# Cutting the second half's projection units and the first half's output units in two pieces, one beside each self-attention step

## The reference

```python
h = _rms(x, w_ln1)
q = (h @ wq + bq).reshape(B, S, N_HEADS, HEAD_DIM)
k = (h @ wk + bk).reshape(B, S, N_KV, HEAD_DIM)
v = (h @ wv + bv).reshape(B, S, N_KV, HEAD_DIM)
q, k = _rope(q, k)
scores = jnp.einsum('bqhd,bkhd->bhqk', q, k) * HEAD_DIM ** (-0.5)
scores = jnp.where(causal[None, None], scores, jnp.finfo(scores.dtype).min)
attn = jax.nn.softmax(scores, axis=-1)
ctx = jnp.einsum('bhqk,bkhd->bqhd', attn, v).reshape(B, S, N_HEADS * HEAD_DIM)
x = x + ctx @ wo
h = _rms(x, w_ln2).reshape(B * S, H)
logits = h @ w_router
```

## Time and profile before

| what | us |
|---|---|
| median of 3 runs | 965.73 |
| lowest and highest of them | 959.88, 966.84 |
| span of the profiled execution | 962.0 |
| TensorE busy with matmuls in it | 902.7 (94%) |
| VectorE, ScalarE, GpSimd busy | 635.9, 561.5, 401.5 |

### The profile page before, as it was taken

One profiled execution on the slowest core, in us unless ns is written; L12 is line 12 of the kernel. 1 busy time (PEld: TensorE's weight loads), 2 busy tenths in 40 slices (PEclk: granted clock), 3 DMA queues, 4 the chain that ended last, 5 costly groups with the idle time before them and its releaser, 6 DMA issues.

```text
span 962.0 us, 16220 instructions
## 1 busy us (share of the span) xinstructions
PE 902.7 (94%) x5759; PEld 836.1 (87%) x5759; DVE 635.9 (66%) x1438; ACT 561.5 (58%) x1448; POOL 401.5 (42%) x382
## 2 busy tenths in 40 slices
PE   5999999999999999999989889799998999998997
PEld 4889999999999999999867767598998888987997
DVE  3557777743537777761597965575866777978764
ACT  3666666754546667663335666545437767776761
POOL 3532222335442223245535323344224766676531
PEclk9999999999999999999999899799989989999999
DMA  5734710016540000005532112134376989998975
GB/s 154 210 88 115 212 51 2 12 39 173 153 125 1 17 1 2 1 12 144 143 94 56 44 48 53 37 98 124 101 250 188 299 244 287 296 303 271 285 191 156
DMA packets 112760, 122.20 MB, mean 127 GB/s; under 512 B 9887, under 2 KB 77927, under 8 KB 112680
## 3 DMA queue, kind: packets, MB, share of 16 engines
q1 hardware_dynamic: 97806, 98.80, 33.4%
q0 software_dynamic: 5184, 12.13, 6.1%
q10 hardware_dynamic: 9690, 10.24, 3.7%
HBM read 110.72 MB, written 19.07 MB: 135 GB/s over the span
## 4 chain that ended last, share of the span: by engine, by line
PE 68%; DVE 13%; DMA 10%; ACT 4%; issue 3%; POOL 2%; ACTq 0%; POOLq 0%; DVEq 0%; SPq 0%
PE bank L2068 61%; PE bank L2197 4%; DMA s_sum<-yo,target 2%; DVE we L1342 2%; DMA eraw<-in_L_ffn_w_up_e_dram 2%; DMA eraw<-in_L_ffn_w_down_e_dram 2%; DMA raw<-in_L_xattn_Wq_dram 1%; ACT we L915 1%; POOL wx L1909 1%; DMA sums<-s_sum 1%; PE bank L2374 1%; DVE PQ L1339 1%; DMA eraw<-in_L_ffn_w_gate_e_dram 1%; DVE wf L1342 1%; DMA raw<-in_L_xattn_Wo_dram 1%
## 5 line engine op out<-in xcount | busy, mean ns | idle before, releaser
L1938 POOL TENSOR_SCALAR SC<-SC,mx,anyv 100x361 f32<-100x361 f32 x128 | 81.8, 651 | 210.4 <-DVE mx L1454 200.6
L1909 POOL TENSOR_TENSOR wf<-raw,wf 128x512 fp32r<-128x512 f32 x54 | 71.6, 1333 | 111.4 <-ACT wf L901 111.4
L1909 POOL TENSOR_TENSOR wx<-raw,wx 128x512 fp32r<-128x512 f32 x64 | 83.4, 1313 | 75.5 <-ACT wx L901 75.2
L1342 DVE TENSOR_TENSOR we<-eraw,we 128x704 fp32r<-128x704 f32 (+2 forms) x100 | 92.1, 938 | 24.6 <-ACT we L915 24.5
L915 ACT ACTIVATE we<-eraw 128x704 fp32r<-128x704 f32 (+2 forms) x140 | 96.3, 718 | 19.9 <-DMA eraw<-in_L_ffn_w_down_e_dram 9.2
L1921 POOL TENSOR_TENSOR we<-eraw,we 128x704 fp32r<-128x704 f32 x40 | 76.3, 1908 | 54.5 <-ACT we L915 54.4
L2068 PE MATMUL bank<-H2h,wf 128*128 128x400 f32 x352 | 99.0, 347 | 0.0
L1031 ACT ACTIVATE SC<-SC,mx 100x361 f32<-100x361 f32 x128 | 75.4, 593 | 28.8 <-DVE mx L1450 27.9
L2068 PE MATMUL bank<-XTh,wx 128*128 128x400 f32 x256 | 71.6, 353 | 3.5 <-POOL wx L1909 2.1
L1342 DVE TENSOR_TENSOR Kl<-bank,Kh 128x362 fp32r<-128x362 f32 x64 | 34.1, 534 | 60.3 <-ACT Kh L989 60.3
L1342 DVE TENSOR_TENSOR QOl<-bank,QOh 128x200 fp32r<-128x200 f32 (+1 forms) x96 | 41.4, 432 | 47.3 <-ACT QOh L944 37.2
(11 more groups left out here) (282 smaller groups left out, 2769.0 us busy)
## 6 DMA issues: line engine op xcount, KB each, us to landing
raw<-s_unit SPq DMA_DIRECT2D x60, 256.0 KB, 3.1
eraw<-in_L_ffn_w_gate_e_dram SPq DMA_DIRECT2D x40, 352.0 KB, 3.9
eraw<-in_L_ffn_w_up_e_dram SPq DMA_DIRECT2D x40, 352.0 KB, 5.4
eraw<-in_L_ffn_w_down_e_dram SPq DMA_DIRECT2D x40, 256.0 KB, 5.9
raw<-in_L_xattn_Wq_dram SPq DMA_DIRECT2D x32, 256.0 KB, 3.0
raw<-in_L_xattn_Wo_dram SPq DMA_DIRECT2D x32, 256.0 KB, 3.0
eraw<-in_L_ffn_w_down_e_dram SPq DMA_DIRECT2D x20, 192.0 KB, 4.9
s_unit<-in_L_ffn_w_sh_gate_dram SPq DMA_DIRECT2D x11, 256.0 KB, 3.7
```

Source lines behind the costliest of these rows:

```text
L1342: return eng.tensor_tensor(o, src, f32(hi), ALU.subtract)
L1909: eng.tensor_tensor(w[:, 1, :, :], raw[plan.raw[stream, u] % 4][:, :, :], f32(w[:, 0, :, :]), ALU.subtract).then_inc(sem("pool_w"), 1)
L1938: eng.tensor_scalar(sc, sc, m[:, 3, h:h + 1], anyv[:, b:b + 1], ALU.mult, ALU.mult).then_inc(sem("pool_p"), 1)
```

## The change

The eight query and key units and the four value units of the second half, and the four output units of the first half, are each issued in two pieces: `..._begin` takes the weights and the bank and makes the first 6 of the 12 matmuls, the old name the other 6 and the signal. Only TensorE has work in the new steps. The pieces stand beside the attention steps like this: units 0 to 3 of query and key still whole behind steps 0 to 3 (the rope of the one before between the pieces); first pieces of units 4, 5, 6, 7 behind 4, 6, 8, 10, second pieces behind 5, 7, 9, 11; rope as before. Value units: first pieces behind 13, 15, 16, 18, second pieces behind 14, 15, 17, 19. Output units: first pieces behind 20, 22, 24, 26, second pieces behind 21, 23, 25, 27. The epilogue is moved and pressed together: `er` two behind 28 and two behind 29, `eroot` and two `erms` behind 30, `eh` behind 31, 32, 33 and 34, router product and first gate unit behind 34, so that only step 35 is left. The `fetch` steps of query and key units 4 to 7 stand one step earlier; those of the value units stand behind 13, 15 and (two) 19, instead of 13, 14 and (two) 17.

```diff
@@ steps_ffn
     at = [[("at", n)] for n in range(8 * HB + 4)]
-    qk = [g for n in range(8) for g in ([fetch, ("qk", 1, n)], [("rope", 1, n)])]
-    yield from take(at, 1)
-    yield from take(qk, 1)
-    for n in range(12):
+    qk = []
+    for n in range(8):
+        qk += [[fetch, ("qk_begin", 1, n)] + ([("rope", 1, n - 1)] if n else []), [("qk", 1, n)]]
+    qk.append([("rope", 1, 7)])
+    for n in range(13):
         yield from take(at, 1)
-        yield from take(qk, 2 if n < 3 else 1)
-    yield from take(qk)
-    v = [[("vbat", 0), fetch], [("vadd", 0), ("vbat", 1), fetch], [("vadd", 1), ("vbat", 2)], [("vadd", 2), ("vbat", 3)],
-         [("vadd", 3), fetch, fetch]]
-    for _ in range(5):
+        yield from take(qk, 2 if n < 4 else 1)
+    v = [[("vbat_begin", 0), fetch], [("vbat", 0)], [("vadd", 0), ("vbat_begin", 1), fetch], [("vbat", 1)],
+         [("vadd", 1), ("vbat_begin", 2)], [("vbat", 2)], [("vadd", 2), ("vbat_begin", 3)], [("vbat", 3)]]
+    for n in range(7):
         yield from take(at, 1)
-        yield from take(v, 1)
-    yield from take(at, 2)
-    po = [[fetch, ("po", 0, m)] for m in range(KD)]
+        yield from take(v, 2 if n == 2 else 1)
+    yield from (("vadd", 3), fetch, fetch)
+    po = [g for m in range(KD) for g in ([fetch, ("po_begin", 0, m)], [("po", 0, m)])]
     ep = epilogue_groups(0)
-    for _ in range(4):
+    for _ in range(8):
+        yield from take(at, 1)
         yield from take(po, 1)
+    for n in range(7):
         yield from take(at, 1)
-    for _ in range(9):
-        yield from take(ep, 1)
-        yield from take(at, 1)
+        yield from take(ep, 2 if n < 2 else 1)
     yield ("moe0",)
@@ tensor_program
+        def qk_begin(n):
+            w, bank = unit("f"), free_bank(("qk", 1, n))
+            begun.append((w, bank))
+            pe.wait_ge(sem("dve_ht"), B)
+            for k in range(2):
+                mm3(bank[:, 0:HT], w[:, 0, k, :], w[:, 1, k, :], HTh[1][:, k, :], HTl[1][:, k, :], k == 0, False)
+
+        def qk_end():
+            w, bank = begun.pop()
+            for k in range(2, KD):
+                e = mm3(bank[:, 0:HT], w[:, 0, k, :], w[:, 1, k, :], HTh[1][:, k, :], HTl[1][:, k, :], False, k == KD - 1)
             e.then_inc(sem("pe_qk"), 1)
+        def v_batch_begin(i):
...
+            v_part(i, bank, range(2))
+
+        def v_batch(i):
+            v_part(i, banks[plan.bank["vbat", i]], range(2, KD)).then_inc(sem("pe_fv"), 1)
+        def po_begin(m):
+            w = unit("f")
+            pe.wait_ge(sem("dve_cx"), HB)
+            bank = free_bank(("po", 0, m))
+            begun.append((w, bank))
+            po_part(0, w, bank, range(2))
```

More of the change, by code:

```diff
@@ L2272, in free_bank, with qk @@
             return banks[plan.bank[key]]
-        def qk(h, n):
+        def qk(n):
             w = unit("f")
-            pe.wait_ge(sem("dve_ht"), HB * (h + 1))
-            if h:
-                bank = free_bank(("qk", h, n))
-            else:
[L2280 to L2284, removed]
-            for k in range(KD):
-                e = mm3(bank[:, 0:HT], w[:, 0, k, :], w[:, 1, k, :], HTh[h][:, k, :], HTl[h][:, k, :], k == 0, k == KD - 1)
+            pe.wait_ge(sem("dve_ht"), HB)
+            bank = banks[n % 4]
+            if n >= 4:
+                pe.wait_ge(sem("dve_rope"), n - 3)
+            else:
+                pe.wait_ge(sem("act_yt"), KD + (n - 2) % 4 + 1)
+            for k in range(KD):
+                e = mm3(bank[:, 0:HT], w[:, 0, k, :], w[:, 1, k, :], HTh[0][:, k, :], HTl[0][:, k, :], k == 0, k == KD - 1)
+            e.then_inc(sem("pe_qk"), 1)
+        begun = []
+        def qk_begin(n):
[8 more added lines that the diff above has]
+                e = mm3(bank[:, 0:HT], w[:, 0, k, :], w[:, 1, k, :], HTh[1][:, k, :], HTl[1][:, k, :], False, k == KD - 1)
             e.then_inc(sem("pe_qk"), 1)
@@ L2306, in tensor_program, with v_part @@
         v_units = []
-        def v_batch(i):
+        def v_part(i, bank, ks):
+            ts = slice(i * T, (i + 1) * T)
+            for k in ks:
+                (name, value), w = v_units[k]
+                pe.wait_ge(sem(name), value)
+                e = mm3(bank[0:T, :], HTh[1][:, k, ts], HTl[1][:, k, ts], flat(w[:, 0, :, :]), flat(w[:, 1, :, :]),
+                        k == 0, k == KD - 1)
+            return e
+        def v_batch_begin(i):
             if i == 0:
@@ L2312, in v_batch @@
             bank = free_bank(("vbat", i))
-            ts = slice(i * T, (i + 1) * T)
             pe.wait_ge(sem("dve_ht"), B)
[L2315 to L2319, removed]
+            v_part(i, bank, range(2))
+        def v_batch(i):
+            v_part(i, banks[plan.bank["vbat", i]], range(2, KD)).then_inc(sem("pe_fv"), 1)
         def f_scores(q, pair):
@@ L2384, in self_attention, with po_part @@
                 f_scores(n // 4 + 1, 0)
+        def po_part(h, w, bank, ks):
+            for k in ks:
+                e = mm3(bank[:, 0:HT], w[:, 0, k, :], w[:, 1, k, :], CXh[h][:, k, :], CXl[h][:, k, :], k == 0, k == KD - 1)
+            return e
+        def po_begin(m):
[4 more added lines that the diff above has]
+            po_part(0, w, bank, range(2))
         def po(h, m):
+            if h == 0:
+                w, bank = begun.pop()
+                po_part(0, w, bank, range(2, KD)).then_inc(sem("pe_po"), 1)
+                return
             w = unit("f")
             pe.wait_ge(sem("dve_cx"), HB * (h + 1))
[L2389 to L2392, removed]
+            po_part(h, w, free_bank(("po", h, m)), range(KD)).then_inc(sem("pe_po"), 1)
         def er(h, i):
@@ L2542, in tensor_program @@
                 resid(*a)
+            elif name == "qk" and a[0] == 0:
+                qk(a[1])
+            elif name == "qk_begin":
+                qk_begin(a[1])
             elif name == "qk":
-                qk(*a)
+                qk_end()
             elif name == "rope" and a[0] == 0 and a[1] - 1 in BY_PE:
@@ L2548, in tensor_program @@
                 v_row(*a)
+            elif name == "vbat_begin":
+                v_batch_begin(*a)
             elif name == "vbat":
@@ L2552, in tensor_program @@
                 self_attention(*a)
+            elif name == "po_begin":
+                po_begin(a[1])
             elif name == "po":
```

## The result

| | before | changed |
|---|---|---|
| median of 20 runs, us | 966.18 | 969.62 |
| span of the profiled execution, us | 962.0 | 967.2 |
| ratio to before, 95% interval | | 1.0045 [1.0026, 1.0063] |

The change makes the kernel slower by 0.45%, some 4 us. I had forecast a gain of 2.8 us.

The account below looks back on a forecast made before the run. VectorE was taken to bound the rotary steps, two-step loops through ScalarE to set the pace after. Terms -7.6+0.6+4.2 gave -2.8 us, from a median of 965.73 to 963.0 us; range 956 to 971.

Parts of the forecast that it names:

- part 1: Query and key units, steps 0 to 12: VectorE stays the bound, halving them loses 0.6 us, bounds 0 and 1.8.
- Parts 2 and 3: Halved value and output units: steps 15 to 26 take 33.4 us, so step 27 starts 7.6 us early.
- 559.7: Forecast start of step 15 in us, against 561.20 before, with step 14's scores starting at 557.0 behind rope.
- the sign that was named for it: Scores of steps 18, 22 and 26 begin 2.4 us behind the odd step's transposes if the forecast is right.
- Part 4: Epilogue pressed into steps 28 to 34: last context product loses 4.2 us, bounds 2.6 and 7.6.
- the hole: TensorE gap of 5 to 10 us forecast in steps 29 to 31, ended by VectorE's copy.
- T: Start of step 27, from which the tail was counted; the router's matmuls were forecast 22.6 us behind it.
- The sum: Net change at the last context product: -7.6+0.6+4.2 = -2.8 us; as the likeliest case 963.0 us, chance 0.45.
- (b): Idle of 1.7 us ahead of step 14's scores brings TensorE's low clock, costing 3.4: 966.3 us; chance 0.25.
- Its price of 3.4: Forecast cost in us of a stretch like 574 to 581 us run at half rate.
- (d): Filler halves too thin: TensorE falls to the low clock in steps 17 to 27 and stays, 976 us; chance 0.06.

Follow-up runs that it names:

- e1: Changed kernel with the rotary step put ahead of the fetch again, all cuts kept; ratio 0.9921 to the kernel before.
- e2: Kernel before, all units whole, only the query and key fetches moved ahead of the rotary step as in the changed kernel; ratio 1.0055.
- e3: Changed kernel with query and key units whole and in the old order, other cuts and pressed epilogue kept; ratio 0.9950 to the kernel before.
- e5: e4 with whole output units on odd steps 21 to 27 and the changed kernel's pressed epilogue; ratio 0.9925 to the kernel before.
- e4: Kernel before, all units whole, value units on odd steps, outputs behind 20 to 23, epilogue one step later; ratio 0.9902.
- e6: e4 with the router product and first gate unit one step later, behind step 34; ratio 0.9880 to the kernel before.

## Why the prediction was wrong, point by point

**The step that failed is part 1.** It said that "only ScalarE, GpSimd and the DMA queue prepare weights a step earlier, with room", and took a loss of 0.6 us, at most 1.8. It counted the step earlier and not what the fetch was moved past: in GpSimd's queue, the rotary product of the unit before. The room was there (GpSimd is busy 19.23 of 41 us) and of no use, as in an ordered queue it is the place that counts. Measured: step 13 comes 8.0 us later, with 7.0 us of waits of VectorE for GpSimd. e1 took 6.4 of it back by that order alone, with no wait for GpSimd left; e2, with the order and no cut, was 11.6 late, some of it by a low clock that fell early. Of the 8.0, 1.4 came by the clock, which had fallen behind the wait ahead of step 12 (step 12 took 3.06 us, 1.68 before). The remaining 1.5 in e1 goes with the cut: there part 1 had the mechanism right (half of unit 5 ahead of the first context product, 2.17 us at the low clock) and took 0.6 where 1.1 to 1.5 came, within its bound of 1.8. All the bounds of part 1 had been made from the cut.

**Parts 2 and 3 were right, as lengths from step 15 on.** From step 15 to step 27 the sum was 33.4 and the changed kernel took 34.0 (569.76 to 603.76), pair by pair 7.25, 5.22, 5.81, 4.95, 5.82 and 4.95 against 7.17, 5.14, 5.70, 4.85, 5.70 and 4.85: a tenth for each switch, as said. The scores of steps 18, 22 and 26 began 2.40 us behind the odd step's transposes each, the sign that was named for it. The start was off by part 1: "559.7" was 569.76, of which 2.3 is this profile's later stage. Step 14's scores did not begin right behind the rotary addition as forecast: the addition ended at 564.92 and the scores began at 566.98, behind transposes and half a value unit that were late by the wait ahead of step 12 and ran at the low clock. In e3, which has the old order up to there, the forecast came true: counted from the first scores, step 14's scores began at 44.2 us (forecast 44.3) and step 15 at 47.1 (47.0).

**Part 4 was right.** Loss 4.2 predicted; from step 27 to the last context product 29.6 against 24.9 us, so 4.7, and the hole stood where it was said, in three gaps before the context product of step 31 (1.15, 1.23 and 2.96), the last ended by VectorE's copy. The router began at T+23.3, not 22.6. That the pressing is the cause shows in the table: kernels with it need 29.6 to 30.5 us for the tail (changed, e1, e3, e5), those without 23.4 to 25.9.

**The sum with part 1 corrected.** 8.0 instead of 0.6 makes -2.8 into +4.6; the stage shows +5.0 to +5.5 (118.40 against 113.37 or 112.87), the timed ratio +4.3.

**Rivals.** (b) came about in its effect and by another way: the clock was 0.54 from 559 to 566, but behind the 3.53 us for which TensorE idled ahead of step 12's transposes; ahead of step 14's scores there was no gap. It cost about 2 us: from step 12's transposes to step 15's are 9.3 us (560.50 to 569.76), in e1, with the same instructions on TensorE at a clock of 1.00, 7.3 (557.33 to 564.65). Its price of 3.4 for a stretch like 574 to 581 was too high as well, e2 puts it at 2.4. (d) did not come: steps 15 to 26 stayed at 1.00, with gaps of 0.17 to 0.43 us ahead of the scores of steps 18, 22 and 26. The Trainium skill's rule on small idles between groups ("TensorE: Matmul & The Clock Gate", section "A second HAM failure mode: psum-queue depth-cycling") is not borne out by these filled steps. In the tail the clock fell (0.71 from 603.76 to 633.39), with gaps of 1.15, 1.23 and 2.96 us. The other side that I should have named is the one that came: a queue that the moved fetch was put ahead of.

**What is not settled.** Behind the last context product the kernels run the same code and still differ: from there to the span's end before took 336.4 us in both profiles, e2 335.0, e4 334.0, e6 336.9, and with the pressed epilogue the changed kernel 333.8, e1 332.2, e3 333.1, e5 335.8. The granted clock of the experts' stretches shows it, before first and then changed:

```profile
700.00:760.00 60.00, 56.10 (x314) 53.85 (x314) 41.32 (x58) 34.36 (x59) 27.68 (x18) 0.94 0.75 237
760.00:820.00 60.00, 54.86 (x289) 50.52 (x288) 43.78 (x60) 41.64 (x74) 37.98 (x22) 0.91 0.90 276
```

```profile
700.00:760.00 60.00, 56.07 (x323) 54.02 (x322) 43.04 (x68) 33.50 (x59) 23.25 (x15) 0.97 0.68 220
760.00:820.00 60.00, 55.17 (x302) 50.08 (x301) 49.00 (x64) 42.54 (x75) 41.27 (x25) 0.97 0.96 290
```

(The changed kernel comes to this code 7.8 us later; counted from the last context product, 74.4 to 134.4 and 134.4 to 194.4 us behind it, the clocks are 0.94 and 0.91 before, 0.97 and 0.97 changed.) This is part of why e1 and e4 came out better in time than their stage says (e1: 1.9 us less than before's second profile inside the stage, 6 to 8 us less in time). In the first of the two stretches so counted all four kernels with the pressed epilogue have 0.97 and all five profiles without it 0.94, so the order of the epilogue may carry on there; in the second both kinds have 0.94 as well as 0.97, and the lengths above overlap. How much is the stage's doing and how much is chance stays open. What e1 gains over the kernel before by its stage alone is 1.4 to 1.9 us.

## What to carry to other kernels

When a step is moved in a list that all engines share, write out for every queue what it was behind and what it is behind now; an engine with half its time free still hands on its work in order. Here one subtraction of 1.3 us that waits for ScalarE, put ahead of a product on the critical loop, made VectorE wait 1.0 to 3.0 us in five places. In a pipeline with a fixed loop time, work fills a hole up to the hole's size and costs its length elsewhere: find which steps have the hole before cutting work into even pieces. Short chained vector work that stood under such waits should stay spread.

## What the runs showed of the hardware that I had not expected

The low clock does not follow from the order of the work alone. The kernel before has two gaps of 1.55 and 1.28 us in steps 18 and 20, and its clock was 0.51 and 0.54 behind them in two profiles; e2 has the same steps with the same gaps and stayed at 1.00, which made steps 19 and 20 2.4 us shorter. e4 and e2 showed 0.66 in the first 10 us of the stage, all others 1.00, though e4's list is the old one there. The same code of the experts' part ran up to 4.7 us faster or slower between kernels (332.2 to 336.9 us) at granted clocks of 0.91 to 0.97 in one stretch. Gaps of 0.17 to 0.43 us once in every 10 us or so, by contrast, never brought it down: 590 to 605 us stayed at 1.00.
